# Parameter loads issued by GpSimd, row copies ahead of the next tiles, and a half wait for the first unit: a 512-sequence pooling and mixture-of-experts kernel on one core

## What is computed

```python
mask = x.sum(-1) != 0
scores = jnp.where(mask, jnp.einsum('bld,d->bl', x, aw), -jnp.inf)
p = jax.nn.softmax(scores, axis=-1)
feature = jnp.einsum('bl,bld->bd', p, x)
g_h = relu(einsum('bd,hdk->bhk', feature, gW1) + gb1)
gate = softmax(einsum('bhk,hke->bhe', g_h, gW2) + gb2)[arange(b), D]
h1 = relu((einsum('bd,edk->ebk', feature, eW1) + eb1) * inv1 + bn1_b)
h2 = relu((einsum('ebk,eko->ebo', h1, eW2) + eb2) * inv2 + bn2_b)
rep = einsum('be,ebo->bo', gate, h2)
out = softmax((einsum('bo,hoc->bhc', rep, hW) + hb)[arange(b), D])
```

## Time and profile before

| | |
|---|---|
| median of three runs | 601.56 us |
| the profiled execution | 601.48 us |
| its span, first to last instruction | 599.7 us |
| PE (TensorE matmul) busy | 509.0 us, 85% |
| DVE busy | 482.8 us, 81% |
| ACT busy | 455.3 us, 76% |
| POOL busy | 81.3 us, 14% |
| DMA | 168.05 MB, mean 280 GB/s |
| granted TensorE clock, mean | 0.956 |

### The profile page before, as it was taken

One profiled execution on the slowest core, in us unless ns is written; L12 is line 12 of the kernel. 1 busy time (PEld: TensorE's weight loads), 2 busy tenths in 40 slices (PEclk: granted clock), 3 DMA queues, 4 the chain that ended last, 5 costly groups with the idle time before them and its releaser, 6 DMA issues.

```text
span 599.7 us, 11283 instructions
## 1 busy us (share of the span) xinstructions
PE 509.0 (85%) x4191; PEld 416.2 (69%) x4191; DVE 482.8 (81%) x961; ACT 455.3 (76%) x1007; POOL 81.3 (14%) x118
## 2 busy tenths in 40 slices
PE   0456555746999999999998989999999999999995
PEld 0111121212978787887777878889999999999995
DVE  6989999997899898888999999475376766667664
ACT  5989999996899888988999986555545665665651
POOL 0000000001112020210111111111211222221200
PEclk9987897698899999999999989999999999999998
DMA  8999999989999999999899944455555566566520
GB/s 315 400 364 402 401 401 401 389 337 385 405 392 395 386 391 394 385 385 354 326 346 347 334 118 155 123 182 157 175 160 155 172 190 193 166 191 187 170 81 0
DMA packets 52339, 168.05 MB, mean 280 GB/s; under 512 B 4797, under 2 KB 5041, under 8 KB 52285
## 3 DMA queue, kind: packets, MB, share of 16 engines
q1 hardware_dynamic: 36012, 100.88, 44.1%
q0 software_dynamic: 16128, 66.07, 33.6%
q10 hardware_dynamic: 144, 0.39, 0.2%
HBM read 167.32 MB, written 0.00 MB: 279 GB/s over the span
## 4 chain that ended last, share of the span: by engine, by line
PE 52%; DVE 23%; DMA 11%; issue 8%; ACT 4%; SPq 1%; ACTq 0%; DVEq 0%
DVE prod_out L626 15%; PE z_ps L875 14%; PE z_ps L876 14%; PE z_ps L877 14%; DMA xring<-in_r_x_dram 11%; PE feat_ps L937 4%; PE z_ps L906 4%; DVE wlo L614 3%; ACT copy_out L429 2%; ACT whi L414 2%; DVE h_hi L682 1%; DVE score L626 0%; SPq L355 0%; DVE h L702 0%; DVE feat_lo L661 0%
## 5 line engine op out<-in xcount | busy, mean ns | idle before, releaser
L626 DVE CUSTOM_DVE_ANT_0 prod_out<-xring,aw_bc 128x768 bf16<-128x768 f32 x256 | 233.2, 947 | 7.1 <-DMA xring<-in_r_x_dram 6.5
L429 ACT ACTIVATE copy_out<-xring 128x768 bf16<-128x768 f32 x256 | 212.6, 832 | 10.3 <-DMA xring<-in_r_x_dram 9.3
L875 PE MATMUL z_ps<-feat_hi,whi 128*128 128x256 f32 x720 | 207.3, 288 | 2.5 <-DVE feat_lo L661 1.2
L876 PE MATMUL z_ps<-feat_lo,whi 128*128 128x256 f32 x720 | 204.3, 284 | 0.0
L877 PE MATMUL z_ps<-feat_hi,wlo 128*128 128x256 f32 x720 | 204.2, 284 | 0.0
L614 DVE TENSOR_TENSOR wlo<-wraw,whi 128x1152 fp32r<-128x1152 f32 x106 | 143.4, 1353 | 74.5 <-ACT whi L414 73.0
L414 ACT ACTIVATE whi<-wraw 128x1152 fp32r<-128x1152 f32 x106 | 122.8, 1158 | 56.9 <-PE z_ps L877 56.1
L875 PEld LDWEIGHTS z_ps<-feat_hi,whi 128*128 128x128 f32 x720 | 139.0, 193 | 4.0 <-DVE feat_lo L661 1.6
L876 PEld LDWEIGHTS z_ps<-feat_lo,whi 128*128 128x128 f32 x720 | 138.8, 193 | 0.0
L877 PEld LDWEIGHTS z_ps<-feat_hi,wlo 128*128 128x128 f32 x720 | 138.7, 193 | 0.0
L937 PE MATMUL feat_ps<-xring,pwin 128*32 128x384 f32 x1024 | 108.4, 559 | 19.6 <-ACT pwin L447 19.6
(11 more groups left out here) (102 smaller groups left out, 325.9 us busy)
## 6 DMA issues: line engine op xcount, KB each, us to landing
xring<-in_r_x_dram SPq DMA_DIRECT2D x128, 768.0 KB, 8.1
wraw<-in_L_rec_eW_dram POOLq DMA_DIRECT2D x90, 576.0 KB, 4.5
wraw<-in_L_rec_gW_dram POOLq DMA_DIRECT2D x16, 576.0 KB, 4.2
w2raw<-in_L_rec_eW_dram POOLq DMA_DIRECT2D x6, 576.0 KB, 7.4
aw_bc<-in_L_rec_aw_dram ACTq DMA_DIRECT2D x1, 384.0 KB, 5.6
w2raw<-in_L_rec_gW_dram SPq DMA_DIRECT2D x1, 48.0 KB
h<-in_L_rec_eb_dram SPq DMA_DIRECT2D x1, 24.0 KB
h<-in_L_rec_bn_g_dram SPq DMA_DIRECT2D x1, 24.0 KB
```

Source lines behind the costliest of these rows:

```text
L429: nc.scalar.activation(copy_out[:, t % 2, :], xring[:, r % RING_ROUNDS, j, i, :], ACT.Copy, accum_out=rowsum[:, r % 2, t:t + 1]).then_inc( ...
L626: nc.vector.tensor_tensor_reduce(out=prod_out[:, t % 2, :], in0=xring[:, r % RING_ROUNDS, j, i, :], in1=aw_bc[:, :], scale=1.0, scalar=0.0 ...
L875: nc.tensor.matmul(psum_tile, w_hi, a_hi, start=first, stop=False)
L876: nc.tensor.matmul(psum_tile, w_hi, a_lo, start=False, stop=False)
```

## The change

The twelve parameter loads leave SP's queue and are issued by GpSimd, ahead of its weight loads, after DVE has scored two tiles. At the end of the first half four things move: `set_params` is parted, its first part (`copy_head_params`) goes behind `softmax_max(15)` and the rest behind `softmax_norm(15)`; `turn_scores(15)` goes from the middle of `add_features(14)` to after its first quarter; `copy_rows(1)` goes ahead of the three tiles of round 16 on ACT and on DVE, and two of the three tiles go behind the features; and unit 0 waits for three of the four feature pieces, unit 1 for the fourth. So that unit 0's first outputs don't fall on transposed features that are still read, these go to banks 2 and 3 of `z_ps` instead of 0 and 1.

```diff
         def turned_feat(b, g):
-            return (z_ps if b < CB else feat_ps)[:, g, 0:KU * P]
+            return z_ps[:, ZB - 2 + g, 0:KU * P] if b < CB else feat_ps[:, g, 0:KU * P]
...
-            for r in range(RING_ROUNDS):
-                load_round(r)
-
-            sp.wait_ge(zeroed, 1)
-            for a, at, src in ((0, 0, eb1), (0, N1, bn1_g), (0, 2 * N1, eb2), (1, 0, bn1_b), (1, N1, bn2_g),
-                               (1, N1 + N2, bn2_b), (1, N1 + 2 * N2, gb1)):
-                src = src.rearrange("e (m p) -> (e m) p", p=P)
-                sp.dma_start(prm_rows[at:at + src.shape[0], a, :], src).then_inc(prm_loaded, 16)
...
-            for r in range(RING_ROUNDS, ROUNDS):
+            for r in range(ROUNDS):
                 load_round(r)
...
+            pool.wait_ge(zeroed, 1)
+            pool.wait_ge(scored, 2)
+            for a, at, src in ((0, 0, eb1), (0, N1, bn1_g), (0, 2 * N1, eb2), (1, 0, bn1_b), (1, N1, bn2_g),
+                               (1, N1 + N2, bn2_b), (1, N1 + 2 * N2, gb1)):
+                src = src.rearrange("e (m p) -> (e m) p", p=P)
+                pool.dma_start(prm_rows[at:at + src.shape[0], a, :], src).then_inc(prm_loaded, 16)
...
-            sum_rows(FIRST_ROUNDS, to_score(0))
             copy_rows(1)
+            sum_rows(FIRST_ROUNDS, to_score(0)[:1])
             for g in range(2):
                 features_hi(1, g)
+            sum_rows(FIRST_ROUNDS, to_score(0)[1:])
...
             mask_scores(FIRST_ROUNDS - 1)
+            softmax_max(FIRST_ROUNDS - 1)
+            copy_head_params()
+            softmax_norm(FIRST_ROUNDS - 1)
             set_params()
-            softmax_max(FIRST_ROUNDS - 1)
-            softmax_norm(FIRST_ROUNDS - 1)
             split_lo(0)
             split_lo(1)
-            score_tiles(FIRST_ROUNDS, to_score(0))
             copy_rows(1)
+            score_tiles(FIRST_ROUNDS, to_score(0)[:1])
             for g in range(2):
                 features_lo(1, g)
+            score_tiles(FIRST_ROUNDS, to_score(0)[1:])
...
-                add_features(r, r + 1 if r + 1 < FIRST_ROUNDS else None)
+                add_features(r, r + 1 if r + 1 < FIRST_ROUNDS else None, (0, 1) if r + 2 == FIRST_ROUNDS else (1, 0))
...
-                if s in (gate_at(c) for c in range(NCH)):
-
-                    pe.wait_ge(feat_ready, 2 * CB * (UNITS[s][0] + 1))
+                for c in range(NCH):
+
+                    if s - gate_at(c) in (0, 1):
+                        pe.wait_ge(feat_ready, 2 * CB * (c + 1) - 1 + s - gate_at(c))
```

More of the change, by code:

```diff
@@ L374, in _ @@
                                     base=0, pattern=[[-1, P]], channel_multiplier=1).then_inc(ident_ready, 1)
+            pool.wait_ge(zeroed, 1)
[4 more added lines that the diff above has]
+                pool.dma_start(prm_rows[at:at + src.shape[0], a, :], src).then_inc(prm_loaded, 16)
+            pool.dma_start(D_i.bitcast(I32), D.rearrange("(b p) -> b p", p=P)).then_inc(prm_loaded, 16)
+            pool.dma_start(gW2_rows, gW2.rearrange("h (m p) e -> (h m) (p e)", p=P)).then_inc(prm_loaded, 16)
+            pool.dma_start(hW_rows, hW.rearrange("h (m p) c -> (h m) (p c)", p=P)).then_inc(prm_loaded, 16)
+            pool.dma_start(gb2_bc[:, :, :], gb2.partition_broadcast(P)).then_inc(prm_loaded, 16)
+            pool.dma_start(hb_bc[:, :, :], hb.partition_broadcast(P)).then_inc(prm_loaded, 16)
             for u in range(SLOTS):
@@ L774, in gate_set, with copy_head_params @@
                                         ALU.subtract).then_inc(gateT_ready, 1)
-            def set_params():
+            def copy_head_params():
                 dve.wait_ge(prm_turned, 1)
@@ L783, in set_params @@
                                             ALU.is_equal)
+            def set_params():
                 nc.vector.tensor_copy(prm[:, 0, 0:2 * N1 + N2], turn_ps[:, 0:2 * N1 + N2])
@@ L920, in turn_probs, with add_features @@
                                     ident[:, :]).then_inc(prob_turned, 1)
-            def add_features(r, between=None):
+            def add_features(r, between=None, turn_at=(1, 0)):
                 pe.wait_ge(pwin_ready, r + 1)
@@ L931, in add_features @@
                 for i in range(2):
-                    if i and between is not None:
-                        turn_scores(between)
                     at = WIN - (4 * in_block + 2 * i)
                     for half in range(2):
+                        if between is not None and (i, half) == turn_at:
+                            turn_scores(between)
                         for j in range(CG):
```

## The result

The change made the kernel faster: 597.77 us, median of four runs (597.32 to 598.24), against 601.49 (600.58 to 602.04, four runs); the ratio is 0.9938, interval 0.9922 to 0.9954. The span, from the first to the last instruction of the profiled execution, fell from 599.7 to 595.9 us. One run of supply_sp, further down, took 669.54 us at a mean granted clock of 0.74, against 0.95 to 0.96 in its five others, and is left out of its median.

The account below looks back on a forecast made before the run. Behind the first half ACT, PE and DVE in turn are nearly full, so an earlier start is carried to the end. From 601.48 us, less 0.8 (loads), 0 (softmax) and 2.5 (copies, half wait): 598.2 us, range 595.7 to 600.9.

Parts of the forecast that it names:

- The loads: Parameter loads at 36 to 42 us: DVE's 2.15 us of waits for x go, 1.3 come back; gain 0.8 us.
- the slower rival: Rounds 1 to 3: GpSimd's work on the twelve loads holds up DVE's scoring; 605.8 us, chance 0.07.
- The softmax of round 15: End of first half: maximum can start at 139.05, but TensorE's features are in the way; gain nothing, ends -0.3 to 0.8 us.
- Row copies and half wait: End of first half: unit 0 starts 2.8 us earlier (2.2 order, 0.6 half wait); 2.5 us counted at 183 us.
- x too late: From 157 to 203 us: x isn't fed sooner, so the second part gains nothing; 600.7 us, chance 0.12.
- Lost later: Stretches up to 352 us: the gain is lost where the bound changes, only 0.5 us arrives; 601.0 us, chance 0.09.

Follow-up runs that it names:

- supply_sp: supply with the twelve parameter loads back on SP's queue; 597.85 us, ratio 0.9938.
- copies_only: Kernel before with only copy_rows(1) put ahead of round 16's three tiles, two of them behind the features, on ACT and DVE; 599.31 us, ratio 0.9968.
- mid_sp: turn_mid with the twelve parameter loads back on SP's queue; 598.30 us, ratio 0.9955.
- loads_only: Kernel before with only the twelve parameter loads moved to GpSimd; 600.95 us, ratio 0.9996.
- supply: turn_mid with GpSimd's first four weight loads each issued one load of x sooner; 596.30 us, ratio 0.9918.
- supply_early: supply with round 15's scores transposed after the first quarter of round 14's features, as in the change; 597.44 us, ratio 0.9934.
- full_wait: Changed kernel with unit 0 waiting for all four feature pieces again; 598.24 us, ratio 0.9955.
- after_again: Changed kernel measured once more, unaltered, on another chip; 598.07 us, ratio 0.9949.
- turn_mid: Changed kernel with round 15's scores transposed back in the middle of round 14's features; 597.72 us, ratio 0.9947.
- params_whole: turn_mid with all of set_params in one piece ahead of softmax_max(15); 598.21 us, ratio 0.9942.

## Why the prediction was right, and which of its terms were not

The time (598.2 forecast, 597.77 measured) and the sum (3.3 us, against 3.1 carried to 352 us in the profiled run) hold. Two terms don't, and their errors nearly cancel against the third, so that the sum came out this close is in part luck. So is the time: from before to after the medians differ by 3.7 us, and in the two profiles 1.05 us of the difference is a stretch at the lower clock that the prediction doesn't have, less 0.4 us at the end of the kernel (the last section).

- **The loads, 0.8.** As far as DVE the mechanism is right: 2.15 us of waits went, some 1.2 came back (1.3 forecast), and round 15 was masked 0.69 us earlier. The other profiles give less. In the eight with one set of loads on GpSimd round 15 is masked from 137.50 to 137.72 (mean 137.60), with 1.2 to 1.9 us of waits for x between 10 and 60 us; in the four with the loads on SP (before, copies_only, mid_sp, supply_sp) from 137.84 to 138.41 (mean 138.13), with 1.8 to 2.2. So moving the loads is worth some 0.5 us at DVE, and 0.8 was high even there. Scoring did not grow, so the slower rival is out; the lock that the Trainium skill describes (SBUF — State Buffer, section "SBUF: two separate sides"), for a DVE instruction with two SBUF inputs only against a GpSimd instruction that reads SBUF, doesn't show in this trace, with 0.95 to 0.96 us for a tile beside GpSimd's issues and 0.94 to 0.96 away from them. But the sum then added these 0.8 us to the end, and loads_only shows none of them there: TensorE gave them away over rounds 14 and 15, in the lower clock. The Trainium skill's rule (DMA: Bandwidth & Descriptors, section "Issuing engines are not separate DMA queues"), read as no gain from the loads, agrees with the time of loads_only, if not by its reason: the waits did shrink. Up to 0.9 us arrive in the one pair of profiles in which x doesn't hold them up (supply_sp against supply).
- **The softmax of round 15, 0 (between a loss of 0.3 and a gain of 0.8).** Mis-sized, and outside its range. The maximum came right behind the mask, as said. But the 0.69 us at the mask were 0.11 at the end of round 15's features, so 0.6 us were lost there. I counted 3.25 us (1.23 + 2.02) for the 24 records behind the mask and hoped for the clock of before; they took 3.84, after 0.76 us of idling. In the other three profiles with this order they took 3.10, 3.32 and 4.07 (supply_early, full_wait, after_again), so the count lay in the middle; between the mask and round 15's features, set against before, these three gained 0.05 us and lost 0.18 and 0.98. Loads and softmax together brought 0.1, not 0.8.
- **Row copies and half wait, 2.5.** The mechanism is right in each step: copies at 145.55 (145.65 forecast), TensorE idle 0.77 us ahead of the transposition (0.7) and 0.77 ahead of unit 0, ACT's wait for unit 0 gone. From the features' end to unit 0 it is 3.12 us shorter (2.8 forecast), 2.65 of it by the copies, as copies_only has it (2.2 forecast). Unit 0 itself comes 3.23 us earlier (3.5 forecast). I had priced two `feat_hi` at 1.13 us and two `feat_lo` at 1.20; they took 0.90 and 1.02. Unit 3's weights are 3.13 us earlier on ACT and 2.55 on DVE, and DVE's idle time took the difference, so 3.0 of the 3.1 carried belong here. Of the two parts, the half wait is 0.47 us (0.6 forecast).
- **x too late.** It did not decide this kernel: no wait of DVE or ACT for x between 150 and 200 us. But it was near, nearer than the chance of 0.12 says: copies_only, full_wait, turn_mid and params_whole, whose leads are 3.6 to 4.3 us, lose 0.7 to 2.2 of them, with waits for x and weights. The change's lead of 3.1 stayed just below.
- **Lost later.** No: 3.13 us at 156 us, 3.12 at 229.
- **Two slips in the working.** The forecast's band, 596.8 to 599.6, doesn't take all ends of its terms: these give 595.8 (2.15, 0.8 and 2.7) to 600.0 (0, a loss of 0.3, and 1.8). And the DMA share isn't 1 or more wherever x is loaded: from 130 to 138 us it is 0.76 in the changed kernel, the hole that supply fills.

The split between the parts is read from single profiles, and loads_only and copies_only bear it out in the time; which piece brings the third to a half of the gain that copies_only lacks, the times don't show, as no other piece taken out alone makes a clear difference. That the lower clock in round 14 is caused by TensorE's waits there is only argued, since the same order was granted different clocks in different runs.

## What to carry to other kernels

Put what an engine downstream waits for (here two copies of 0.5 us) ahead of work that only fills time; with the half wait that was nearly the whole lead in the profiled run, and alone it gave between half and two thirds of the gain in time. A gain at one engine is worth what the next one passes on: follow it to the place where all engines are full before it is added to a sum. When a lead is won, the supply is the next cap: look for a hole in the transfers ahead of it, and issue there what is needed later.

## What was not expected of the hardware

Ten of the fourteen profiles have, at about 320 us or at about 350, some 3.5 us at the lower clock; the other four, the changed kernel's among them, have none. At both places TensorE stands idle first: it waits up to 2.06 us for DVE's normalised weights of a round. The kernel before (the last wait ahead of its fall), and the changed kernel (the same wait, with no fall behind it):

```profile
351.57 0.33 PE L919 MATMUL soft_ps<-ident,prob 128*128 128x128 f32 x1 [2.06 <-DVE prob L649]
```

```profile
348.45 0.33 PE L925 MATMUL soft_ps<-ident,prob 128*128 128x128 f32 x1 [2.06 <-DVE prob L651]
```

All ten stretches begin within some 1.5 us behind such a wait of 2.06 us. Of the 24 waits of this length at the two places in the fourteen profiles, 14 are not followed by one, so the wait alone doesn't decide it; what does is open. What a stretch costs depends on where it falls. The kernel before, the changed kernel, and turn_mid:

```profile
352.00:356.00 4.00, 4.00 (x24) 4.00 (x23) 3.97 (x8) 3.96 (x10) 0.76 (x1) 0.57 0.43 122
```

```profile
352.00:356.00 4.00, 4.00 (x45) 2.22 (x45) 3.97 (x9) 4.00 (x8) 0.76 (x1) 1.00 0.35 132
```

```profile
320.00:324.00 4.00, 4.00 (x23) 4.00 (x22) 3.97 (x8) 3.96 (x10) 0.76 (x1) 0.58 1.04 389
```

At 320 us, where DVE sets the pace, it costs nothing: turn_mid's lead is 3.67 us on both sides of it. Behind 352 us TensorE's 4.00 us do the work of some two at the full clock (24 records against 45), and the kernel before loses 1.05 us there, which the changed kernel's profiled run doesn't. That is why the spans differ by 3.8 us and the lead at 229 us by 3.1 (0.4 us is lost again at the very end, where the changed kernel's last matmuls get a lower granted clock, 0.74 from 588 to 590 us). Single runs of one kernel differ by as much, so a difference of one microsecond needs many runs, or a profile read at the place of the edit.
